# Latent attention: keys turned by a DMA transfer, score units in four groups of three, row rotation on VectorE

## What is computed

```
kv_rope = kv_c * cos + rotate_half(kv_c) * sin        # 1500 rows x 64 of each batch
scores  = q_r @ k_r.T                                  # 16 heads x 56 tokens against 1500 rows
attn    = softmax(scores)
ctx_c   = attn @ kv_rope                               # 64 wide for each head and token
out     = (ctx_c @ w_kc_kv) @ Wo.T
```

## Time and profile before

| what | value |
|---|---|
| time, median of 3 runs | 1811.01 us (1799.75 to 1813.59) |
| the profiled execution | 1797.95 us |
| its span in the trace | 1796.2 us |
| TensorE, VectorE, ScalarE, GpSimd busy | 1431.9, 1361.9, 1053.4, 652.1 us |
| the latent loop in it | about 354 to 961 us |

### The profile page before, as it was taken

The page is one execution under the profiler, slowest core; times in us unless marked ns, Lnnn a source line. Parts: engine busy times, 40 slices in busy tenths (PEclk is TensorE's granted clock), DMA queues, the critical chain, the costliest instruction groups (busy, mean ns, idle before and its releaser), DMA issues. The chain is left out here.

```text
span 1796.2 us, 40092 instructions
## 1 busy us (share of the span) xinstructions
PE 1431.9 (80%) x13869; PEld 917.4 (51%) x13884; DVE 1361.9 (76%) x2397; ACT 1053.4 (59%) x1795; POOL 652.1 (36%) x658
## 2 busy tenths in 40 slices
PE   1687776899999999999997754992778699945992
PEld 0455553444444444444444743991566567634891
DVE  6888875699988888889886784547898656576774
ACT  1767763577677777777773243551676555454461
POOL 1212213165455465554630145562333200037241
PEclk9856665999999999999998857996899989968996
DMA  6950000111221212222110225444000000034335
GB/s 138 315 165 1 1 1 35 38 36 49 61 59 49 72 48 60 60 48 72 48 45 7 60 74 161 157 148 128 1 1 0 1 2 1 1 96 141 107 102 164
DMA packets 106444, 123.65 MB, mean 69 GB/s; under 512 B 23553, under 2 KB 87625, under 8 KB 106211
## 3 DMA queue, kind: packets, MB, share of 16 engines
q1 hardware_dynamic: 96451, 98.87, 20.5%
q0 software_dynamic: 7776, 21.28, 3.2%
q10 hardware_dynamic: 2112, 2.10, 0.4%
HBM read 66.85 MB, written 40.30 MB: 60 GB/s over the span
## 5 line engine op out<-in xcount | busy, mean ns | idle before, releaser
L2824 DVE TENSOR_TENSOR lat_dsum<-lat_dsum,lat_Pb 125x896 f32<-125x896 f32 x320 | 477.3, 1492 | 67.4 <-ACT lat_Pb L2739 58.5
L2739 ACT ACTIVATE lat_Pb<-banks 125x896 f32<-125x896 f32 x384 | 329.0, 927 | 141.2 <-PE banks L2617 114.8
L2595 PE MATMUL banks<-lat_Pb,lat_kv 125*64 125x448 f32 x1536 | 306.4, 541 | 0.0
L2617 PE MATMUL banks<-lat_Q,lat_kT 64*125 64x448 f16 x2304 | 258.8, 360 | 4.2 <-DVE lat_QT L2785 1.3
L2617 PEld LDWEIGHTS banks<-lat_Q,lat_kT 64*125 64x125 f16 x2304 | 142.6, 134 | 149.3 <-issue 66.9
L2595 PEld LDWEIGHTS banks<-lat_Pb,lat_kv 125*64 125x64 f32 x1536 | 100.6, 137 | 146.4 <-issue 137.6
L2534 POOL TENSOR_TENSOR lat_kk<-lat_rot,lat_kk 125x768 f16<-125x768 f32 x32 | 65.8, 2057 | 279.3 <-ACT lat_kk L2696 279.3
L3165 POOL DMA_INDIRECT sent_outputs<-moe_yb,moe_yidx x98 | 95.6, 975 | 115.5 <-ACT moe_yb L3424 100.5
L3303 PE MATMUL banks<-moe_w2d,moe_gT 88*128 (+3 forms) x780 | 100.0, 278 | 17.6 <-DVE moe_gT L3642 13.7
L3630 DVE COPY moe_xTb<-banks 128x1024 f16<-128x1024 f16 x49 | 33.9, 691 | 76.8 <-PE banks L3270 76.8
L3303 PEld LDWEIGHTS banks<-moe_w2d,moe_gT 88*128 88x128 f16 (+1 forms) x780 | 75.5, 99 | 30.1 <-issue 19.7
(11 more groups left out here) (450 smaller groups left out, 3111.8 us busy)
## 6 DMA issues: line engine op xcount, KB each, us to landing
lat_Q<-lat_QT SPq DMA_DIRECT2D x128, 112.0 KB, 3.4
moe_xb<-sent_rows SPq DMA_DIRECT2D x49, 257.0 KB
lat_raw<-in_ctx_dram SPq DMA_DIRECT2D x32, 375.0 KB
sent_rows<-zero SPq DMA_DIRECT2D x1, 7453.0 KB, 39.8
lat_rD<-lat_reciprocals SPq DMA_DIRECT2D x62, 112.0 KB, 2.8
moe_arena<-sent_outputs SPq DMA_DIRECT2D x12, 512.0 KB, 7.5
sent_rows<-zero SPq DMA_DIRECT2D x1, 5140.0 KB, 57.6
sent_outputs<-zero SPq DMA_DIRECT2D x1, 4096.0 KB, 41.6
```

The lines of the kernel that those rows point to most:

```text
L2595: ins = nc.tensor.matmul(ps[u * DC:(u + 1) * DC, 6, 0:8 * T], kv[:, par, tt, :], Pb[:, tile_slot(tt, par), u, :], start=tt == 0, stop=tt = ...
L2617: ins = nc.tensor.matmul(ps[0:KP, n % 3 * 2 + q, 0:8 * T], kT[rows, par, 2 * pair + low, 0:KP], Q2[rows, par, w, 8 * u:8 * u + 8, :].rearr ...
L2739: nc.scalar.activation(Pb[:, slot:slot + 2, u, :], ps[0:KP, n % 3 * 2:n % 3 * 2 + 2, 0:8 * T], ACT.Exp, scale=1.0 / QSCALE).then_inc(exp_d ...
L2824: ins = nc.vector.tensor_tensor(dsum[:, par], dsum[:, par], Pb[:, tile_slot(tt, par)], ALU.add)
```

## The change

Each engine's program for the latent loop is edited, in these parts:

1. TensorE no longer transposes keys and ScalarE no longer evacuates them. SP issues one transposing transfer for each batch, `kk` [128, 12 x 128] to `kT`, behind the low part of the keys (`kl_made`) and ahead of `spread_reciprocals`. `kk` has 128 partitions instead of 125 and the block width KS is 128 instead of 126; GpSimd zeroes partitions 96 to 127 of `kk` once.
2. The score units come in four groups of three. Behind them stand the values of four, two, three and three tiles: behind group 0 tiles 8 to 11 of the batch before; behind group 1 its denominators (one group later than before) and tiles 0 and 1; then 2 to 4, and 5 to 7.
3. From batch 2 on VectorE rotates the rows and makes the low part. GpSimd does so for batches 0 and 1 only. The rotation for b + 2 stands behind the sum of tile 8, the low part for b + 1 behind the sum of tile 2.
4. On VectorE the reciprocals of the batch before move from behind tile 6 to behind tile 9. The product of context and reciprocals moves from behind tile 10 to behind tile 1 of the batch after, with `pv` in two buffers. Batch 30's product stands behind the loop.
5. On ScalarE the high part of the next keys moves from behind unit 3 to behind unit 2, keeping the context from ahead of unit 4 to ahead of unit 3, keeping the denominators from behind unit 4 to behind unit 5.

The diff, cut to its core:

```diff
-KS = 126
+KS = 128
@@ SP, body(b, par)
+                        sp.wait_ge(kl_made, b + 1)
+                        sp.sem_inc(turn_begun, 1)
+                        sp.dma_start(kT[:, par], kk[:, par].rearrange("p t d -> p (t d)"),
+                                     transpose=True).then_inc(kT_in, 16)
                         if past(b, 2):
                             spread_reciprocals(b - 2)
@@ GpSimd
+                    nc.gpsimd.memset(kk[96:P], 0.0).then_inc(rests_zeroed, 1)
...
-                    over_tiles(pool, body, 0, s, 3, n=B)
+                    for b in range(2):
...
@@ TensorE
                     def denominators(b, par):
                         pe.wait_ge(summed, (b + 1) * (KT - 1))
-                        pe.wait_ge(kT_made, min(b + 1, B - 1) * NTURN + 2 if isinstance(b, int)
-                                   else b * NTURN + (NTURN + 2))
+                        if past(b, 1):
+                            pe.wait_ge(den_kept, b)
...
+                        pe.wait_ge(kT_in, 16 * b + 16)
+                        pe.wait_ge(spread[par], 4 * half_count(b, par))
+                        for g, tiles in enumerate((range(-4, 0), range(0, 2), range(2, 5), range(5, 8))):
+                            for n in range(3 * g, 3 * g + 3):
+                                scores(b, par, n // 2, n % 2)
+                            if g == 1 and past(b, 1):
+                                denominators(b - 1, (par + 1) % 2)
+                            for tt in tiles:
+                                if tt >= 0:
                                     values(b, par, tt)
                                 elif past(b, 1):
                                     values(b - 1, (par + 1) % 2, KT + tt)
@@ ScalarE
-                            if n == 4 and past(b, 1):
-                                keep_context(b - 1)
+                            if n == 3 and past(b, 1):
+                                keep_context(b - 1, (par + 1) % 2)
...
-                            if n == 3:
-                                evacuate(b, par, 1)
-                                if live(b + 1, B):
-                                    high(b + 1, (par + 1) % 2)
+                            if n == 2 and live(b + 1, B):
+                                high(b + 1, (par + 1) % 2)
...
-                            if n == 4 and past(b, 1):
+                            if n == 5 and past(b, 1):
                                 keep_denominators(b - 1)
-                            if n == 10 and live(b + 1, B):
-                                evacuate(b + 1, (par + 1) % 2, 0)
@@ VectorE
+                    def kept_context(b, par):
+                        dve.wait_ge(pv_kept, b + 1)
+                        dve.wait_ge(rec_in, 32 * b + 32)
+                        context(b, pv[:, par])
+
+                    def rotated_rows(b, par):
+                        r = raw[:, par]
+                        dve.wait_ge(raw_in[par], half_count(b, par))
+                        dve.wait_ge(rotated, b)
+                        dve.wait_ge(kv_made, b - 1)
+                        dve.wait_ge(kl_made, b - 1)
+                        nc.vector.tensor_tensor(rot[:, par], r, cosK[:], ALU.mult
+                                                ).then_inc(products_made, 1)
+                        nc.vector.tensor_tensor(rot2[:, :, 0:Q], r[:, :, Q:DC], sinK[:, :, 0:Q],
+                                                ALU.mult).then_inc(products_made, 1)
+                        nc.vector.tensor_tensor(rot2[:, :, Q:DC], r[:, :, 0:Q], sinK[:, :, Q:DC],
+                                                ALU.mult).then_inc(products_made, 1)
+                        dve.wait_ge(products_made, 3 * b - 3)
+                        nc.vector.tensor_tensor(rot[:, par], rot[:, par], rot2[:], ALU.add
+                                                ).then_inc(rotated, 1)
+
+                    def low(b, par):
+                        dve.wait_ge(kh_made, b + 1)
+                        nc.vector.tensor_tensor(halves(par, True), paired(rot[:, par]),
+                                                halves(par, False), ALU.subtract).then_inc(kl_made, 1)
...
-                            if tt == 6 and past(b, 1):
+                            if tt == 1 and past(b, 2):
+                                kept_context(b - 2, par)
+                            if tt == 2 and past(b, 1) and live(b + 1, B):
+                                low(b + 1, other)
+                            if tt == 9 and past(b, 1):
                                 reciprocals(b - 1)
-                            if tt == KT - 2 and past(b, 1):
-                                dve.wait_ge(pv_kept, b)
-                                dve.wait_ge(rec_in, 32 * b)
-                                context(b - 1, pv[:])
-
-                    over_tiles(dve, body, 0, n=B)
+                            if tt == 8 and live(b + 2, B):
+                                rotated_rows(b + 2, par)
+
+                    over_tiles(dve, body, 1, n=B)
+                    kept_context(B - 2, 0)
```

More of the change, by code:

```diff
@@ L2390, in halves @@
             def halves(par, low):
-                return kk[:, par, low:KT:2, :]
+                return kk[0:KP, par, low:KT:2, :]
             def paired(a):
@@ L2566, in queries_of @@
                             ins.then_inc(q_done, 1)
-                    def turn(b, par, c):
-                        pe.wait_ge(kl_made, b + 1)
-                        if c == 1:
-                            pe.wait_ge(kT_made, b * NTURN + 1)
-                        elif past(b, 2):
-                            pe.wait_ge(den_kept, b - 1)
-                        pe.sem_inc(turn_begun, 1)
-                        bank = ps[:, 7, :].bitcast(F16)
-                        for tt in range(8 * c, min(8 * c + 8, KT)):
-                            n = tt - 8 * c
-                            for q in range(2):
-                                rows = slice(q * DC, (q + 1) * DC)
-                                ins = nc.tensor.transpose(
-                                    bank[rows, n * KS:n * KS + KP],
-                                    kk[:, par, tt, rows], id16[0:KP, 0:KP])
-                        ins.then_inc(kT_done, 1)
                     def values(b, par, tt):
@@ L2634, in body @@
                             return
-                        for g in range(3):
-                            if g == 0:
-                                pe.wait_ge(kT_made, b * NTURN + 1)
-                                pe.wait_ge(spread[par], 4 * half_count(b, par))
-                            if g == 2:
-                                pe.wait_ge(kT_made, b * NTURN + 2)
-                            for pair in (2 * g, 2 * g + 1):
-                                for u in range(2):
-                                    scores(b, par, pair, u)
-                            if g == 0:
-                                turn(b, par, 1)
-                            if g == 2 and live(b + 1, B):
-                                turn(b + 1, (par + 1) % 2, 0)
-                            for tt in range(4 * g - 4, 4 * g):
-                                if g:
+                        pe.wait_ge(kT_in, 16 * b + 16)
[7 more added lines that the diff above has]
+                                if tt >= 0:
                                     values(b, par, tt)
@@ L2652, in body @@
                                     values(b - 1, (par + 1) % 2, KT + tt)
-                            if g == 0 and past(b, 1):
-                                denominators(b - 1, (par + 1) % 2)
                     over_tiles(pe, body, 1, n=B)
```

65 lines of the change are left out of this document (26 added, 39 removed).

## The result

The changed kernel takes 1788.51 us (median of 4 runs, 1781.82 to 1792.83), the kernel before 1809.50 us in the runs beside it (1799.75 to 1813.59). The ratio is 0.9894 with a 95% interval of 0.9854 to 0.9934: 1.1% faster, which is 19 us (21 by the two medians), where 15 were forecast. The profiled executions, 1797.95 us before and 1791.94 after, differ by only 6 us. A second set of four runs on another chip gave 0.9893 (0.9840 to 0.9947). All ratios here are of fast runs; of the experiments' runs one, of the keys in two transfers, was slow (5289.74 us).

What follows compares the result with a forecast made beforehand. VectorE, held by the reciprocals' round trip, was to bound the loop: 12.75 us of work plus 5.55 of trip, 18.3 a batch against 18.88. That saves 18 us, less 3 at the end: 1811 - 15 = 1796 us, range 1762 to 1845.

Steps and rivals of the forecast that it cites:

- The wait that decides: VectorE waits 2.3 us a batch for the reciprocals' 5.55 us round trip before their product with the context; period 18.3 us.
- late keys: Rival at the batch's first scores: turned keys land too late and set the period; 1835 us at 11.3 us delay; chance 0.22.
- 16.2 us of VectorE's work: VectorE's need per batch without waits: 11 sums (12.0), rotation 2.76, low half 0.86, product 0.54 and 0.11.
- TensorE after the change: TensorE's need per batch in the latent loop: 18.74 - 0.71 - 1.32 + 0.16 = 16.9, taken as 17.0 us.
- rival A: Faster: the reciprocals' round trip is shorter or covered, 1784 down to 1756 us; chance 0.20 beyond the forecast's own range.
- TensorE busy 93%: Expected sign in the latent loop's trace: TensorE's busy share, 17.0 / 18.3, with TensorE idle 1.3 us a batch.
- rival C: Slower: TensorE, idle 1.3 us a batch, has its clock fall; at 0.8 77 us more, 1888 us; chance 0.04.
- The turning transfer: The transfer that turns the keys before the next batch's scores: taken as 5 us, hidden, binding only beyond 8.8 us.
- rival B: Slower: turned keys land late, deciding from 8.8 us; at 11.3 us 24 us more, 1835 us; chance 0.22.
- Start: Opening batches keep GpSimd's rotation, so the start of the latent loop was to cost nothing.
- End: In the last batch, batch 30's product waits 5.55 us after its reciprocal, ahead of the closing reciprocal: 3 us more.
- Rival D: Exponentials start later and each group of three waits at its head; period near 18.8 us, 1811 us; chance 0.06.

Runs made afterwards that it cites:

- the kernel with both edits: The changed kernel with the reciprocals behind the sum of tile 8 and GpSimd's zeroing behind the split of the output weights: 1766.46 us, ratio 0.9795 to the kernel before.
- second and third set: Sets of experiment runs, each on one chip beside the kernel before, whose median was 1803.91 us in the second, 1806.98 in the third and 1823.25 in the first.

## Why the prediction was right, and where it was not

**The wait that decides: right, and shown.** The forecast made the round trip of the reciprocals the new bound. Covering it by an earlier start or by a later use took the period from 18.41 to 17.65 us in both experiments, with at most 2.6 us of the wait left in the loop and TensorE full. That these runs also brought the keys earlier leaves late keys as a rival, and two things speak against it. VectorE's circle is closed without them: 12.84 us of work and 5.53 of trip are 18.37 of the 18.41, and VectorE waits for exponentials only 4.4 us in the whole loop. And where the trip differs from run to run, the period follows: less the wait for the reciprocals it is 16.03 us in the changed kernel (18.41 - 2.38), 16.03 in its second profile (18.28 - 2.25) and 16.03 with the keys in two transfers (18.15 - 2.12). The forecast's 16.2 us of VectorE's work is this number.

The terms held one by one: 12.84 us of work for 12.75, 5.53 us of trip for 5.55, 2.38 idle for 2.3, and the rotation's operations at 0.95 and 0.55 us for 0.95 and 0.56. They came from slopes and from spacings of starts, and that is what made them good: durations alone would have overstated VectorE's work.

**TensorE after the change: 17.0 forecast, 17.65 measured.** One term of this sum was mis-sized, the 1.32 us of waits that groups of three were to save. These rows of the kernel before belong to the batch of the earlier trace rows:

```profile
668.62 3.23 PE L2595 MATMUL banks<-lat_Pb,lat_kv 125*64 125x448 f32 x16
671.77 2.65 PE L2617 MATMUL banks<-lat_Q,lat_kT 64*125 64x448 f16 x24
674.36 0.63 PE L2582 MATMUL banks<-id,lat_kk 125*64 125x125 f16 x16
674.82 3.18 PE L2595 MATMUL banks<-lat_Pb,lat_kv 125*64 125x448 f32 x16
```

With them both batches can be taken apart by the distances of starts, this one and the one with the trip covered (reciprocals one tile earlier):

| us a batch | before | trip covered | change | forecast |
|---|---|---|---|---|
| scores | 2.67 + 2.66 + 2.59 = 7.92 | 4 x 1.85 = 7.40 | -0.52 | -1.32 |
| transposes | 0.24 + 0.46 = 0.70 | 0 | -0.70 | -0.71 |
| values | 3.01 + 3.15 + 3.11 = 9.27 | 9.58 | +0.31 | +0.16 |
| denominators | 0.85 | 0.80 | -0.05 | 0 |
| sum | 18.74 | 17.78 | -0.96 | -1.87 |

The 0.44 of the earlier trace rows is the idle time of a weight load, and the loads run beside the matmuls: what TensorE lost by the fourth unit in that group was 2.67 - 4 x 0.615 (a third of 1.85) = 0.2. A unit takes 0.615 us, not the 0.56 that was left after taking 0.44 off. The values' term was a little small too, by 0.15 in this batch.

The error did not reach the time, since VectorE's 18.41 stood above it. It would have reached rival A, whose far end (1756) took the 17.0 for TensorE: with the trip wholly covered, the profile gives 31 x (18.88 - 17.65) = 38 us, and the kernel with both edits measured 37.5 less than the kernel before (1803.91 - 1766.46).

**TensorE busy 93%: 97%.** The same error: 17.65 of 18.41 is 96%. The clock stayed at 1.00, so rival C has nothing for it.

**The turning transfer: right on the size, not on the slack.** It took 5.1 us in the median for the 5 taken, under the 8.8 from which rival B decides, so rival B falls. But the step called the transfer hidden, and it is barely that: most batches' first scores start as soon as the keys are there, with waits of about 0.3 us in 10 places. They seem to cost nothing, as the denominators behind them wait for VectorE's sum in any case (14.5 us in the loop), and with the keys in two transfers more of them went with a shorter period. The Trainium skill's "VectorE: DVE Perf Modes" gives 1309 ns for one 128x128 block by DMA; the estimate of 15.7 us for twelve in series is refuted by the landing at 3.7 us at best and 5.1 in the median. The Trainium skill's "Advanced Engine Details and Errata", section X-Bar Transpose (TRN2), is nearer: an estimated 1.1 us of moving by its rate, with 1.43 us of issue at best in the 3.7. But the halves give 0.9 us for 192 KB, which makes some 1.8 us for the whole, above that estimate. The landing also differs with the order around it: with the reciprocals one tile earlier it is 3.7 us in the median too, and the issue 1.49 where it was 2.2.

**Start: nothing forecast, 2.6 us lost** (61.7 for 59.1), of which moving the zeroing brought back 2.1. The step counted GpSimd's rotation of the first batches and passed over the zeroing, one instruction of 2.65 us that runs beside VectorE's normalisations. **End: 3 us forecast, 0.1 measured.** From the last first sum to the last product it is 955.5 - 931.4 = 24.1 us against 966.4 - 942.4 = 24.0. The wait for the last reciprocals is there, 2.78 us, but the last batches have no rotation and no low half to make, and that gives it back; the step left this out.

**Rival D** (each group waits at its head for what the fourth unit waited for) would have kept the period near 18.8. In the changed kernel with the trip covered TensorE has no idle time at all, so it falls.

**What stays open.** From the first sum to the last product the profiles give 609.4 - 594.9 = 14.5 us saved, and with 2.6 lost at the start 11.9; the second profile of the changed kernel gives 18.5 and 15.6 in the same way. The runs give 19 (12 to 26 by the interval). The stages behind the loop, in which no code differs, took 821.6 us in the profile before and 826.4 in the one after, 820.8 to 829.4 in the profiles of the second and third set, and 843.0 to 845.8 in the four of the first, on the chip where the kernel before is slower too. This scatter is of the size of what is missing, and one or two profiles for each kernel can't settle it. Nor has any run the transposes back on TensorE with the rest as changed, so that what the transfer alone brings is read from rows, not from a time. That the 15 of the forecast lies so near the 19 is thus partly luck: the period's share came out near (14.6 us for 18), the start cost 2.6 us that the forecast had not counted, and the end did not cost the 3 us that it had.

## What to carry to other kernels

When work moves onto an engine with spare time, add up not its busy time but its longest circle: work from one use of a remote result to the making of the next, plus the trip of that result. Here it was 12.84 + 5.53 us on an engine 85% busy, and moving the start of the trip ahead of the moved work, one line, gained about as much as the whole change (17.9 us). Before a stall is counted as a saving, take it from the spacing of the stalled engine's own instructions, not from the idle time of a queue that overlaps it; and time what an edit issues once, in the opening, against what runs beside it.

## What the runs showed of the hardware

- A transposing transfer of 384 KB between two places of SBUF lands 3.7 us after the start of its issue at best and 5.1 in the median of the changed kernel, 6.2 (8.2 at most) in another, and 3.7 in the median where the reciprocals go earlier. Half of it lands after 2.8 at best and 4.2 in the median: it isn't nearly twice as fast.
- GpSimd's zeroing of 32 partitions stretches VectorE's four 128 x 256 operations beside it from 1.38 to 3.59 us, though they touch other tiles.
- Shorter groups of scores, which save 0.78 us a batch in the changed kernel's order once VectorE doesn't wait, cost 1.35 in the kernel before: with the denominators one group too early it was 1.9% slower.
- The idle time of a weight load is not TensorE's: 0.44 us of it stood for 0.2 us that the matmuls lost.
